# Softmax attention: one DMA for the peaks, a reciprocal of each head's sums copied through DRAM, routing work in pieces

## The reference

```python
x = x + tanh(g_xattn[0]) * L0_xattn(layernorm(x), ctx, ...)   # the stage that is changed
x = x + tanh(g_ffn[0])   * L0_ffn(layernorm(x), ...)          # 8 experts, 2 per token; its routing is worked out inside the first stage
x = x + tanh(g_xattn[1]) * L1_xattn(...)                      # linear attention
x = x + tanh(g_ffn[1])   * L1_ffn(...)                        # causal attention, 16 experts, 4 per token

def L0_xattn(x, c, ...):      # batch 64, 64 channels, 256 positions, 8 heads of 8 channels
    q, k, v = heads(Wq x + bq), heads(Wk c + bk), heads(Wv c + bv)
    q, k = rotary(q), rotary(k)
    p = softmax(q k^T / sqrt(8))          # 256 x 256 for each head
    return Wo (p v) + bo
```

## Time and profile before

| | |
|---|---|
| median of three runs | 2583.53 us (2583.38 to 2583.6) |
| the profiled execution, its own time | 2571.76 us |
| its span, first to last instruction | 2569.9 us |
| busy share of the span: PE, PEld, DVE, ACT, POOL | 86%, 65%, 71%, 45%, 43% |
| mean granted clock of TensorE | 0.926 of 2.4 GHz |
| softmax stage: first to last reciprocal of the sums (L782) | 93.6 to 631.8 us |
| instructions | 60412 |

### The profile page before, as it was taken

How to read it: one execution, slowest core, us unless ns; L and a number is a source line. 1 busy time by engine, 2 the same in 40 slices (tenths; PEclk the granted TensorE clock), 3 DMA queues, 4 the chain that set the end, 5 groups by cost and what they waited for, 6 DMA issues and landing times. The chain is left out here.

```text
span 2569.9 us, 60412 instructions
## 1 busy us (share of the span) xinstructions
PE 2199.1 (86%) x20880; PEld 1669.5 (65%) x20880; DVE 1835.5 (71%) x3965; ACT 1154.2 (45%) x2509; POOL 1104.7 (43%) x1111
## 2 busy tenths in 40 slices
PE   6889888886878799993899998999988699999990
PEld 4555555543766577762677777777766577888880
DVE  4888988872557787765878878878787374545754
ACT  2677767664534233323444444444333264333330
POOL 3454555565154500002555445455487600334736
PEclk9888989975899899997999999999999799999995
DMA  5455554442469523212332332322334382445854
GB/s 115 108 134 139 149 142 133 118 137 76 126 198 296 150 88 103 77 38 53 82 88 56 83 84 62 84 73 69 79 99 115 123 266 83 139 142 183 265 170 147
DMA packets 250435, 313.10 MB, mean 122 GB/s; under 512 B 45216, under 2 KB 202912, under 8 KB 250144
## 3 DMA queue, kind: packets, MB, share of 16 engines
q1 hardware_dynamic: 189168, 219.11, 30.7%
q0 software_dynamic: 26624, 58.79, 8.2%
q10 hardware_dynamic: 34352, 31.34, 3.6%
HBM read 122.40 MB, written 102.24 MB: 87 GB/s over the span
## 5 line engine op out<-in xcount | busy, mean ns | idle before, releaser
L2126 POOL TENSOR_TENSOR ca_qk<-ca_qk,ca_q_swap 128x512 f32<-128x512 f32 x160 | 248.9, 1556 | 366.6 <-DVE ca_q_swap L2304 366.1
L735 DVE TENSOR_REDUCE soft_top<-soft_pa 128x2 fp32r<-128x512 f32 x512 | 327.9, 683 | 83.0 <-PE soft_pa L816 80.2
L630 ACT ACTIVATE soft_prob<-soft_pb 128x512 f32<-128x512 f32 x512 | 286.1, 594 | 171.3 <-PE soft_pb L809 169.5
L809 PE MATMUL soft_pb<-soft_rep 32*128 32x256 f32 x1024 | 207.3, 359 | 53.2 <-DVE soft_top L735 27.6
L809 PEld LDWEIGHTS soft_pb<-soft_rep 32*128 32x128 f32 x1024 | 135.4, 211 | 170.3 <-issue 73.5
L816 PE MATMUL soft_pa<-soft_rep 31*128 31x256 f32 x1024 | 217.1, 366 | 5.9 <-DVE soft_top L735 3.5
L1459 PE MATMUL moe_py<-moe_w_d,moe_at 128*128 x788 | 212.7, 385 | 1.4 <-issue 0.8
L1440 PE MATMUL moe_pgu<-moe_w_hi,moe_xt_hi 128*128 x472 | 192.8, 408 | 22.7 <-DVE moe_xt_lo L1357 13.0
L2396 PE MATMUL ca_py<-ca_w_hi,ca_ot_hi 128*128 128x256 f32 x512 | 156.7, 306 | 38.3 <-DVE ca_ot_lo L2325 38.0
L1363 DVE TENSOR_TENSOR moe_act_f<-moe_silu,moe_pgu 128x256 f32<-128x256 f32 (+1 forms) x236 | 88.6, 375 | 131.5 <-ACT moe_silu L1258 131.2
L2304 DVE TENSOR_TENSOR ca_q_swap<-ca_q_swap,ca_sin_q 128x512 f32<-128x512 f32 x128 | 117.2, 916 | 82.0 <-DMA ca_q_swap<-ca_q_f 81.7
(11 more groups left out here) (377 smaller groups left out, 6252.7 us busy)
## 6 DMA issues: line engine op xcount, KB each, us to landing
ca_q_swap<-ca_q_f SPq DMA_DIRECT2D x640, 64.0 KB
moe_xs<-moe_rows SPq DMA_DIRECT2D x236, 128.0 KB
soft_rep<-soft_parts SPq DMA_DIRECT2D x378, 64.0 KB
moe_rows<-soft_blank SPq DMA_DIRECT2D x27, 768.0 KB
moe_ys_rows<-moe_ys ACTq DMA_DIRECT2D x134, 128.0 KB, 1.7
moe_ys<-moe_ys ACTq DMA_DIRECT2D x102, 128.0 KB, 2.6
moe_xd<-scratch SPq DMA_DIRECT2D x64, 128.0 KB, 2.7
ca_vs<-ca_v SPq DMA_DIRECT2D x32, 256.0 KB, 3.8
```

The costliest lines, as they stand in the source:

```text
L630: act.activation(prob[:, k % 4, h, :], p_b[:, 2 * T * h:2 * T * (h + 1)], ACT.Exp).then_inc(prob_ready, 1)
L735: dve.tensor_reduce(heads[:, j, :, g], p_a[:, 2 * T * h:2 * T * (h + 1)].rearrange("p (c s) -> p c s", c=HALF), AX, ALU.max).then_inc(a_do ...
L809: mm = pe.matmul(p_b[:, out], rep[of, i % 4, g, at:at + PART], rep[of, i % 4, g, 0:T], start=True, stop=True)
L2126: pool.tensor_tensor(qk[:, u % 2, m, :], qk[:, u % 2, m, :], q_swap[:, p % 2, :], ALU.add).then_inc(qk_ready, 1)
```

## The change

The four DMAs of the peaks become one, from 16 partitions of `soft_peak` to the partitions 31, 63, 95 and 127 of `soft_rep`.

Of the eight copies of each sum only one is packed: one DMA from rows 8, 40, 72 and 104 of `soft_o_raw` to `soft_sums`, now 128 x 32 (each partition takes 32 positions of one head). It is issued before the four DMAs of the outputs. VectorE takes the reciprocal of 128 x 32 behind its sixth pair of maxima (`maxima(i, 5)`) instead of the eighth. POOL stores the result to a DRAM tensor behind the low parts, and in the next iteration, behind the roots, waits for the store, issues four DMAs that read it back with each head's row repeated eight times into `soft_rsum`, waits for them, and multiplies. Only then does it come to the DMAs of the next tile's sums. The product of a tile so moves from the end of iteration t + 1 to the first half of iteration t + 2.

On ScalarE `soft_xn` moves behind `soft_vaug`, `soft_y` moves in front of `exp(i, 7)`, and the router's `scale` comes one iteration later, behind `exp(i, 3)`. `choose` takes two tiles at a time in twice as many iterations, `place` moves behind `maxima(23, 4)`, and `weigh` is split over the iterations 24 to 27.

```diff
-    ROUTED, STRETCH, SENDS = MOE_TILES["moe0"][0], 4, 4
+    ROUTED, STRETCH, SENDS = MOE_TILES["moe0"][0], 2, 4
...
-        packed, sums = sb("packed", [PART, 2, T]), sb("sums", [PART, 2, T])
+        packed, sums = sb("packed", [PART, 2, T]), sb("sums", [PART, 2, HEADS * T // PART])
+        inverse = sb("inverse", [PART, 2, HEADS * T // PART])
...
+        inverse_rows = [nc.dram_tensor(f"soft_inverse{i}", (4, GROUPS, T), fp32, kind="Internal").ap() for i in range(2)]
...
-                        for j in range(4):
-                            at = 32 * j + SPLIT
-                            sp.dma_start(rep[at:at + 1, n % 4, :, 0:T].bitcast(fp32), peak[4 * j:4 * j + 4, n % 2, :].bitcast(fp32)
-                                         ).then_inc(peak_in[n % 2], 16)
+                        sp.dma_start(rep[SPLIT:PART:32, n % 4, :, 0:T].bitcast(fp32), peak[0:HEADS, n % 2, :].bitcast(fp32)
+                                     ).then_inc(peak_in[n % 2], 16)
...
+                    t = i - 2
+                    if live(t):
+                        pool.wait_ge(inverse_out, 16 * (t + 1))
+                        past(pool, on_ready, t)
+                        for j in range(4):
+                            pool.dma_start(rsum[32 * j:32 * j + 32, :], inverse_rows[t % 2][j].unsqueeze(0).to_broadcast([KC, GROUPS, T])
+                                           ).then_inc(rsum_in, 16)
+                        pool.wait_ge(rsum_in, 64 * (t + 1))
+                        pool.wait_ge(pack_in[t % 2], PACK * (t // 2 + 1))
+                        past(pool, wo_ready, t - 1)
+                        pool.tensor_tensor(on[:, t % 2, :], packed[:, t % 2, :], rsum[:], ALU.mult).then_inc(on_ready, 1)
                     t = i - 1
                     if live(t):
                         pool.wait_ge(o_out, GROUPS * (t + 1))
                         past(pool, on_ready, t - 1)
+                        past(pool, inverse_ready, t - 1)
+                        pool.dma_start(sums[:, t % 2, :], o_raw[KC:PART:32, t % 2, :, :]).then_inc(sums_in[t % 2], 16)
                         for j in range(4):
                             to = slice(32 * j, 32 * j + 32)
-                            for row, dst in ((0, packed), (KC, sums)):
-                                pool.dma_start(dst[to, t % 2, :], o_raw[32 * j + row:32 * j + row + KC, t % 2, :, :]
-                                               ).then_inc(pack_in[t % 2], 16)
+                            pool.dma_start(packed[to, t % 2, :], o_raw[32 * j:32 * j + KC, t % 2, :, :]
+                                           ).then_inc(pack_in[t % 2], 16)
...
                     if live(t):
-                        pool.wait_ge(rsum_ready, t + 1)
-                        past(pool, wo_ready, t - 1)
-                        pool.tensor_tensor(on[:, t % 2, :], packed[:, t % 2, :], rsum[:], ALU.mult).then_inc(on_ready, 1)
+                        pool.wait_ge(inverse_ready, t + 1)
+                        past(pool, rsum_in, 64 * (t - 1))
+                        pool.dma_start(inverse_rows[t % 2].rearrange("j g (c q) -> (j g c) q", q=HEADS * T // PART),
+                                       inverse[:, t % 2, :]).then_inc(inverse_out, 16)
...
+                    if i == RANK + 1:
+                        route.place(dve)
...
                     maxima(i, 5)
+                    t = i - 1
+                    if live(t):
+                        dve.wait_ge(sums_in[t % 2], 16 * (t // 2 + 1))
+                        past(dve, inverse_out, 16 * (t - 1))
+                        dve.reciprocal(inverse[:, t % 2, :], sums[:, t % 2, :]).then_inc(inverse_ready, 1)
                     maxima(i, 6)
...
                     if i == RANK + 1:
-                        route.place(dve)
                         route.place_rows(dve)
-                    if i == RANK + 3:
-                        route.weigh(dve)
-                    t = i - 1
-                    if live(t):
-                        dve.wait_ge(pack_in[t % 2], PACK * (t // 2 + 1))
-                        past(dve, on_ready, t)
-                        dve.reciprocal(rsum[:], sums[:, t % 2, :]).then_inc(rsum_ready, 1)
+                    if i == RANK + 2:
+                        route.share(dve)
+                    if i - RANK - 3 in range(route.TOP):
+                        route.share_of(dve, i - RANK - 3)
+                    if i == RANK + 3 + route.TOP:
+                        route.name_experts(dve)
```

More of the change, by code:

```diff
@@ L479, in stage_softmax_attention @@
         b_ready, prob_ready, pv_done, o_out = sem("b"), sem("prob"), sem("pv"), sem("o_out")
-        pack_in = [sem(f"pack{i}") for i in range(2)]
-        rsum_ready, on_ready, wo_ready = sem("rsum"), sem("on"), sem("wo")
+        pack_in, sums_in = ([sem(f"{n}{i}") for i in range(2)] for n in ("pack", "sums"))
+        inverse_ready, inverse_out, rsum_in = sem("inverse"), sem("inverse_out"), sem("rsum_in")
+        on_ready, wo_ready = sem("on"), sem("wo")
         y_ready, xo_ready = sem("y"), sem("xo")
@@ L485, in stage_softmax_attention @@
         NCONST = 6
-        REP, PACK = 16 * 12, 16 * 8
+        REP, PACK = 16 * 12, 16 * 4
         live = lambda n: 0 <= n < TILES
@@ L636, in keep @@
                             past(act, pack_in[t % 2], PACK * (t // 2))
+                            past(act, sums_in[t % 2], 16 * (t // 2))
                         act.activation(o_raw[:, t % 2, g, :], p_o[g % 2][:, 0:T], ACT.Copy).then_inc(o_out, 1)
@@ L645, in _ @@
                     exp(i, 3)
+                    if routed(i - 5):
+                        route.scale(act, i - 5, lambda t: xo[:, t % KEEP, :])
                     if routed(i - 6):
@@ L651, in _ @@
                     n = i + 5
-                    if live(n):
-                        act.wait_ge(low_ready, n + 1)
-                        past(act, qkrot_ready, n - 1)
-                        act.activation(xn[:, n % 2, :], xt[:, n % RING, :], ACT.Identity, bias=low[:], scale=rstd[:]
-                                       ).then_inc(xn_ready, 1)
                     if n in (0, 1, 2):
@@ L662, in _ @@
                     if live(n):
-                        past(act, peak_in[n % 2], 64 * (n // 2))
+                        past(act, peak_in[n % 2], 16 * (n // 2))
                         act.activation(peak[0:HEADS, n % 2, :], p_x[0][0:HEADS, T:2 * T], ACT.Copy).then_inc(peak_ready, 1)
@@ L671, in _ @@
                                        p_x[0][:, 0:T].rearrange("p (n k) -> p n k", k=KC), ACT.Copy).then_inc(vaug_ready, 1)
+                    n = i + 5
+                    if live(n):
+                        act.wait_ge(low_ready, n + 1)
+                        past(act, qkrot_ready, n - 1)
+                        act.activation(xn[:, n % 2, :], xt[:, n % RING, :], ACT.Identity, bias=low[:], scale=rstd[:]
+                                       ).then_inc(xn_ready, 1)
                     exp(i, 6)
                     keep(i, 1)
+                    t = i - 2
+                    if live(t):
+                        act.wait_ge(wo_ready, t + 1)
+                        if t == 0:
+                            act.wait_ge(shift_ready, 1)
+                        past(act, xo_ready, t - 1)
+                        act.activation(y[:, t % 2, :], p_x[1][:, 0:T], ACT.Identity, bias=shift[:], scale=gate[:]
+                                       ).then_inc(y_ready, 1)
                     exp(i, 7)
-                    if routed(i - 4):
-                        route.scale(act, i - 4, lambda t: xo[:, t % KEEP, :])
                     if routed(i - 5):
@@ L795, in both @@
                     if live(i) and k == 0:
-                        pe.wait_ge(peak_in[i % 2], 64 * (i // 2 + 1))
+                        pe.wait_ge(peak_in[i % 2], 16 * (i // 2 + 1))
                     if live(n) and m == 0:
```

8 lines of the change are left out of this document (removed).

## The result

| | before | changed |
|---|---|---|
| median | 2583.45 us (2581.75 to 2583.6, 4 runs) | 2700.7 us (2691.72 to 2704.76, 4 runs) |
| span of the profiled execution | 2569.9 us | 2700.0 us |
| busy share PE, DVE, ACT, POOL | 86, 71, 45, 43% | 83, 66, 43, 42% |
| mean granted clock | 0.926 | 0.895 |
| first and last reciprocal of the sums | 93.59 and 631.82 | 89.34 and 758.02 |

What follows compares the result with a forecast made beforehand. Tensor engine and VectorE hand each other two buffers, neither full, with the reciprocal the longest thing in between. Tiles -10.4 and -4, routing -4 and -0.7, sends +7.3, tail +1: about -11 us, 2572.5 against the median; range 2548 to 2606.

Steps and rivals of the forecast that it cites:

- ScalarE order: Moved ScalarE instructions in the attention tiles: counted at nothing, covered by 3.35 us of ScalarE idle time a tile.
- x: Time from a DMA issue's end to its landing on the sums' path: taken as 1.9 us, bounds 1.64 and 4.95.
- The new path on POOL: Sums' store, loads and product in line: 9.5 + 3x, 15.2 us a tile; full-clock tiles gain 10.4 us, others 4.
- The rival of the wait in the reciprocal's place: VectorE waits for the sums: at x of 2.5, +22 us, 2606; at 3.2, over +50; chance 0.28.
- Reciprocal: VectorE's reciprocal of the sums, cut to 128 x 32: 0.35 us instead of 1.745, 1.4 us less work a tile.
- What that is worth if nothing else waits: Attention tile with the shorter reciprocal and no other wait: 14.9 us instead of 16.02.
- Peaks: Peaks by one DMA: lands before the tensor engine needs it; gains its 0.25 us wait, counted within the tile's gain.
- The sends: Four indirect DMAs on POOL ahead of the next sums: 19.6 us each for iterations 25 to 27, 7.3 us lost.
- Routing in pieces: Half a `choose` fits VectorE's free time at an iteration's end: 4 us won, plus 0.7 for early `place`.
- the tail's loss: After the stage's last product, sums, reciprocal, store and loads in line take 9.5 us: 1 us lost.

Runs made afterwards that it cites:

- e1: The changed kernel with the router's `scale` back in its old place at the end of the iteration; 2630.67 us, 1.017 of the kernel before.
- e10: The changed kernel, late `scale` kept, with the router's root issued behind POOL's loads, product and DMAs of sums and outputs; 2616.93 us, 1.0144 of the kernel before.
- e4: The kernel before with the new path of the sums alone; 2639.77 us, 1.0211 of the kernel before.
- e5: The changed kernel with `scale` in its old place and POOL issuing the next sums and outputs before waiting for the loads; 2568.49 us, 0.9952 of the kernel before.
- e3: The kernel before with every part of the change except the new path of the sums; 2616.35 us, 1.0118 of the kernel before.
- e6: The kernel before with the peaks by one DMA and nothing else; 2576.98 us, 0.998 of the kernel before.
- e7: The kernel before with the routing in pieces (`place` and `weigh` too) and nothing else; 2580.64 us, 0.9997 of the kernel before.
- e2: The kernel before with the router's `scale` one iteration later, behind `exp(i, 3)`, alone; 2590.06 us, 1.0025 of the kernel before.

## Why the prediction was wrong

**The step that failed.** In *ScalarE order* the prediction says "The same instructions" and "I count nothing for it: cover is ScalarE's idle time". It looked at what the moved work costs on ScalarE, and of the three moves it weighed only that of `soft_y`. One of the two left out, `scale` one iteration later, has its price on another engine: POOL's next root waits for the row, and the loads, the product and the sums' DMA stand behind the root. The prediction lists the two roots in the earlier trace rows as 1.1 us of work that lies "under the first x". In the changed kernel the second waits 5.4 to 8.1 us (97.3 in 15). e1 and e10 put this term, which the sum had at nothing, at 70 to 84 of the 117 us. Nothing of this needed the trace of the changed kernel: L166 has the wait for `row_ready`, and the diff moves the instruction that raises it behind `exp(i, 3)`.

**The term that was mis-sized.** *The new path on POOL*, 9.5 + 3x, is a ring that the tiles without a root follow; x, the time from the end of an issue to the landing, was taken at 1.9. In an unrouted tile (the first window above) the legs read:

```profile
114.70 2.18 POOL L591 DMA_DIRECT2D soft_rsum<-soft_inverse  x4
120.36 0.72 POOL L596 TENSOR_TENSOR soft_on<-soft_packed,soft_rsum 128x256 f32<-128x256 f32 x1 [3.48 <-DMA soft_rsum<-soft_inverse]
121.03 0.72 POOL L602 DMA_DIRECT2D soft_sums<-soft_o_raw  x1
```

```profile
126.52 0.35 DVE L787 RECIPROCAL soft_inverse<-soft_sums 128x32 f32<-128x32 f32 x1 [3.99 <-DMA soft_sums<-soft_o_raw]
```

Loads 3.48, sums 126.52 - 121.75 = 4.77, and the store's at most 2.17 (issue ended at 112.53, loads issued at 114.70, with 0.88 of other waiting in between). Then 9.5 + 10.4 = 19.9 us, against 19.12 measured; so x is 3.2 by the window and at most 3.5 by the legs, about the middle of the bounds of 1.64 and 4.95. This tile is not a typical one for the sums' leg: it is one of five in which SP issues the loads of x and ctx near the sums' DMA. Measured in the same way, from the end of POOL's issue to the reciprocal that waited for it, the landing took 4.55 to 5.15 us in these five, and 1.45 to 4.85, with a median of 2.3, in 21 others of the changed kernel. For the loads of the reciprocals POOL waited 90.9 / 32 = 2.8 us on average in the changed kernel and 107.4 / 28 = 3.8 in e1. So both legs that could be measured lie above 1.9 on average, the loads further than the typical sums. The rival of the wait in the reciprocal's place said "At 3.2 it would be over +50", and e4 measured +56. The nearest row was chosen wrongly: the earlier trace rows is a transfer with nothing beside it, and the 0.26 of the earlier trace rows is the DMA share early in an iteration. But the ring itself moves the sums' DMA into the part where SP issues the peaks, a piece of zeros and the loads: 0.9 to 3.2 us behind the sums' DMA in the unrouted tile, from 0.9 us before it in the routed one. POOL's own four DMAs of the outputs follow it at once. The DMA share from the sums' issue to their landing, in the unrouted tile and in the routed one above:

```profile
121.75:126.52 4.77, 2.11 (x28) 0.99 (x26) 0.78 (x3) 3.31 (x9) 3.43 (x6) 1.00 0.78 157
...
338.87:341.18 2.31, 0.10 (x1) 0.00 (x0) 0.00 (x0) 0.76 (x3) 2.31 (x5) 1.00 0.91 300
```

That the other traffic makes x long is argued from this, not shown. The five long landings beside the loads of x and ctx speak for it; against it, at 0.91 a landing took 2.31, and in e1 landings beside such loads took 2.07 to 4.92 and one without them 4.87.

The Trainium skill ("DMA: Bandwidth & Descriptors", Anatomy of one DMA — SWDGE path) gives about 2.0 us for the fixed part. The two landings of the sums just shown took 2.31 and 4.77, both above it, the second by more than twice, so in this place the figure is no measure of a landing beside other traffic. By it the ring is 15.5 us, and the prediction would have been as wrong.

**What held.** *Reciprocal*: 0.352 us measured, 0.35 forecast. *What that is worth if nothing else waits*: 14.9 forecast, and 15.00 measured in the best tiles of e5 once the ring was broken; but the average tile gained 0.3 us there and not 1.1, so that this held for a tile and not for the sum. *Peaks*: the tensor engine's wait for them fell from 12.6 us in 19 to none in the changed kernel and 1.9 in 4 in e3, and e6 gains 0.20% (-0.02 to 0.43); but in e5, with the same single DMA, it is back at 12.7 us in 10. *The sends*: 19.6 us forecast for iterations 25 to 27, and 21.7, 21.6 and 20.8 measured, with VectorE waiting 6.6, 5.4 and 5.0 us before the reciprocal where 4 were forecast. *Routing in pieces* did not hold: 4.7 us forecast, 1 measured (e7), not to be told from none.

**The chances.** The slow rival had 0.28, with its mechanism and its place right; the range had been cut at x of 2.5 although the bound named was 4.95. By that bound the ring is 24.4 us, and the 13 tiles at full clock alone give 13 x 8.4 = 109 us more, 2692. A range that kept it, with the sends' and the tail's loss added, would have taken in the result, though for the wrong reason: 70 to 84 us of it are another wait.

## What to carry to other kernels

When an instruction is moved later, look up who waits for its semaphore, for its result and for its buffer to be free, and then what stands behind that waiter in its queue; the moved instruction's own cost is not the price. A transfer on a path that closes within one iteration is paid in full each time, so an in-order engine should issue the next transfer before it waits for the last: that reordering alone was worth some 60 us here and turned a loss of 1.7% into a gain of 0.5%. For a landing time take the row whose neighbours are those that the transfer will have in its new place, and if none is there, leave the upper bound in the range.

## What the runs showed of the hardware that was not expected

VectorE's operation on one column was held up for as long as a running operation of POOL: L173 took 0.15 us alone and 1.33 us beside POOL's addition of 128 x 512 in e3, with a mean over 16 of 1.04 us in e2 and 0.95 in e3 against 0.22 in the kernel before. The Trainium skill ("SBUF — State Buffer", SBUF: two separate sides) says that a VectorE operation with two inputs in SBUF and a GpSimd operation that reads SBUF take a shared port pair as an exclusive lock, so that the second waits for the whole of the first; L173 reads two tiles in SBUF, and the trace agrees, with 1.33 us for both. What was not expected is that moving a wait on POOL, and none of its work, is enough to bring the two together.

A tensor engine that stood for 3.18 us came back at the lower of its two clock levels: in e3 the sixteen products with the values took 1.94 us at 1.2 GHz behind that wait and 1.07 at 2.4 before it, and the window behind it has a clock of 0.73. Where this happens a wait costs more than itself. But long waits are not the only thing that comes before a fall: in the kernel before the same products took 1.07 us at 199.26 and 1.94 at 204.09, and the tensor engine was busy for 4.51 of the 4.83 us in between. What brings the fall there, the runs don't show.
